# Attention slots of a six-layer windowed block: order, banks and the rotated product

## What is computed

```python
def attn_layer(x, Wqkv, qs, ksc, Wo):              # x shifted by one token in half of its features
    q, k, v = jnp.split(x @ Wqkv, 3, -1)           # 16 heads of 64
    q = l2norm(q) * qs;  k = l2norm(k) * ksc
    q = q * cos * scale + rotate_half(q) * sin * scale
    k = k * cos * inv + rotate_half(k) * sin * inv
    out = local_attention(q, k, v)                 # window 32, looks at itself and the window before
    return out.transpose(0, 2, 1, 3).reshape(b, n, INNER) @ Wo
...
for i in range(DEPTH):                             # DEPTH = 6
    x = attn_layer(shift_tokens(x), ...) + x
    x = ffn_layer(shift_tokens(x), ...) + x
```

## Time and profile before

| | us |
|---|---|
| median of 3 runs | 3929.46 (3925.46 to 3941.01) |
| span of the profiled execution | 3926.6 |
| TensorE matmuls busy | 3690.6 (94%) |
| VectorE busy | 3058.0 (78%) |
| GpSimd busy | 2597.4 (66%) |
| ScalarE busy | 2270.7 (58%) |

### The profile page before, as it was taken

How to read it: one execution, slowest core, us unless ns; L and a number is a source line. 1 busy time by engine, 2 the same in 40 slices (tenths; PEclk the granted TensorE clock), 3 DMA queues, 4 the chain that set the end, 5 groups by cost and what they waited for, 6 DMA issues and landing times.

```text
span 3926.6 us, 163773 instructions
## 1 busy us (share of the span) xinstructions
PE 3690.6 (94%) x67712; PEld 2844.7 (72%) x67712; DVE 3058.0 (78%) x5829; ACT 2270.7 (58%) x4270; POOL 2597.4 (66%) x3029
## 2 busy tenths in 40 slices
PE   5999979999999999999999999999999999999998
PEld 3555557777767777677877678787677876777876
DVE  7666658888778888788887788887788887888876
ACT  3555546666546666456666366665466664566653
POOL 4545538787547887367887288775477873687870
PEclk8999989999999999999999999999999999999999
DMA  1000002222212222122222122222122221222220
GB/s 44 4 6 4 6 28 68 56 60 60 58 32 59 59 57 59 41 49 60 61 57 56 30 65 57 59 61 58 32 60 58 59 56 41 54 57 58 60 52 22
DMA packets 136313, 189.08 MB, mean 48 GB/s; under 512 B 38006, under 2 KB 58484, under 8 KB 135412
## 3 DMA queue, kind: packets, MB, share of 16 engines
q1 hardware_dynamic: 135540, 178.23, 17.7%
HBM read 22.67 MB, written 2.10 MB: 6 GB/s over the span
## 4 chain that ended last, share of the span: by engine, by line
PE 76%; issue 4%; DVE 2%; POOL 2%; ACT 0%; DMA 0%; POOLq 0%; SPq 0%; DVEq 0%; ACTq 0%
PE PS L1270 18%; PE PS L1417 10%; PE PS L1256 10%; PE PS L1294 8%; PE PS L1280 8%; PE PS L1258 8%; PE PS L1257 8%; PE PS L1476 2%; PE PS L1411 2%; PE PS L1454 1%; PE PS L1447 1%; POOL t L1182 1%; PE PS L1442 1%; POOL t L1187 0%; DVE m L1800 0%
## 5 line engine op out<-in xcount | busy, mean ns | idle before, releaser
L1182 POOL TENSOR_TENSOR t<-t 128x1024 f32<-128x1024 f32 x384 | 908.0, 2370 | 363.9 <-DVE t L1762 362.6
L1187 POOL TENSOR_TENSOR t<-t,rn 128x1024 f32<-128x1024 f32 x384 | 723.6, 1905 | 29.8 <-POOL rn L150 27.3
L1542 ACT ACTIVATE va<-PS 128x512 f32<-128x512 f32 x384 | 229.8, 599 | 614.4 <-PE PS L1258 611.6
L1760 DVE TENSOR_TENSOR t<-PS,rope 128x512 f32<-128x512 f32 x768 | 523.2, 681 | 26.1 <-ACT sq L1577 24.5
L1256 PE MATMUL PS<-w_hi,xh 128*128 128x512 f32 x1152 | 514.2, 446 | 22.3 <-DVE xl L1063 11.3
L1577 ACT ACTIVATE sq<-PS 128x512 f32<-128x512 f32 x768 | 454.1, 593 | 33.0 <-PE PS L1258 17.7
L1270 PE MATMUL PS<-constants,t 128*128 128x128 f32 x3072 | 443.8, 277 | 19.8 <-POOL t L1187 12.8
L1258 PE MATMUL PS<-w_lo,xh 128*128 128x512 f32 x1152 | 458.5, 398 | 0.0
L1257 PE MATMUL PS<-w_hi,xl 128*128 128x512 f32 x1152 | 457.5, 397 | 0.0
L1767 DVE TENSOR_REDUCE ss<-sq 128x16 f32<-128x1024 f32 x384 | 448.3, 1209 | 0.0
L1270 PEld LDWEIGHTS PS<-constants,t 128*128 128x128 f32 x3072 | 351.9, 141 | 68.9 <-POOL t L1187 15.9
(11 more groups left out here) (168 smaller groups left out, 7869.8 us busy)
## 6 DMA issues: line engine op xcount, KB each, us to landing
vs<-va SPq DMA_DIRECT2D x768, 130.0 KB
vs<-va SPq DMA_DIRECT2D x768, 65.0 KB
t<-in_L_ffn_Wqkv SPq DMA_DIRECT2D x18, 512.0 KB, 4.4
w_out<-in_L_ffn_Wo SPq DMA_DIRECT2D x6, 512.0 KB, 3.9
a_normed<-in_L_attn_x SPq DMA_DIRECT2D x8, 256.0 KB, 7.0
a_xo<-in_L_attn_x SPq DMA_DIRECT2D x8, 256.0 KB, 2.8
out<-total SPq DMA_DIRECT2D x8, 256.0 KB, 3.5
w_raw<-in_L_ffn_W SPq DMA_DIRECT2D x6, 341.0 KB
```

The costliest lines, as they stand in the source:

```text
L1182: pool.tensor_tensor(mine[:, i, :], mine[:, i, :], t2[:, i, :], ALU.add).then_inc(done, 1)
L1187: pool.tensor_tensor(h, h, bc(rn[:, H * i:H * (i + 1)], 2, HB), ALU.mult).then_inc(done, 1)
L1760: dve.tensor_tensor(o1, src, bc(rope[:, 2 * i, t, :], 1, 8), ALU.mult)
```

## The change

The order on TensorE becomes k0, k1, v0, both halves of `turn_weights`, q0, q1, both of `turn_q`, both value products one behind the other, v1, both of `turn_k`, both of `turn_mixed`, the masks and all scores in one run, and the output projection last. Banks are fixed for each use: v0 in bank 1, v1 in 6, k in 4 and 5, q in 6 and 7, k transposed in 4 and 5, the mixed output transposed in 7 and 6, value products of half 0 in 2 and 3, of half 1 in 0 and 1, the output projection in 0. VectorE adds the output of a tile one slot later, ahead of the rotations, and `rope_half` makes the product with the sines in one operation that reads its source with the two halves of each head swapped (`swapped`). ScalarE's order follows. The diff, indentation reduced:

```diff
@@ -1291,7 +1291,7 @@
                 v = va[rows, room(s, t), par, pair, :] if k is None else vs[rows, t % 2, k, pair, :]
-                last = pe.matmul(PS[W * w:W * (w + 1), (0, 2)[c] + par, HB1 * (pair % 4):HB1 * (pair % 4 + 1)],
+                last = pe.matmul(PS[W * w:W * (w + 1), (2, 0)[c] + par, HB1 * (pair % 4):HB1 * (pair % 4 + 1)],
                                  pT[rows, pair, W * w:W * (w + 1)], v, start=True, stop=True,
@@ -1306,7 +1306,7 @@
     closing, ending = list(ages) == CLOSING, list(ages) == LAST
-    oT_at, y_at = (0, 2) if ending else (4, 4)
+    oT_at = (7, 6) if project_new else (0, 1)
     roped = lambda i: lambda j: t1[:, tile1 % 2, i, P * j:P * (j + 1)]
@@ -1322,41 +1322,47 @@
         pe.wait_ge(kn_made, at(T, 1, 1, 1))
-        if mix:
-            pe.wait_ge(on_made, at(T, 2, 2, 1))
-        turn(c, lambda j: roped(1)(4 * c + j), kt_mm)
+        pe.wait_ge(qT_made, at(T, 1, 2, c + 1))
+        turn(4 + c, lambda j: roped(1)(4 * c + j), kt_mm)
 
     def turn_mixed(c):
-        if score:
-            pe.wait_ge(qT_made, at(T, 1, 2, c + 1))
-        pe.wait_ge(on_made, at(T, 2, 2, c + 1))
-        turn(oT_at + c, lambda j: on[:, 4 * c + j, :, :].rearrange("p r d -> p (r d)"), ot_mm)
+        pe.wait_ge(on_made, at(T, 2, 2, c + 1 if project_new else 2))
+        if project_new and c == 0:
+            pe.wait_ge(rq_made, at(T, 0, 2, 2))
+        if project_new and c == 1:
+            pe.wait_ge(v_made, at(T, 0, 2, 2))
+        turn(oT_at[c], lambda j: on[:, 4 * c + j, :, :].rearrange("p r d -> p (r d)"), ot_mm)
 
     def mix_half(c):
-        pe.wait_ge(pT_made, at(T, 2, 2, c + 1))
+        pe.wait_ge(pT_made, at(T, 2, 2, 2))
+        if c == 1:
+            pe.wait_ge(attn_done, at(T, 3, 1, 1))
+            if project_new:
+                pe.wait_ge(v_made, at(T, 0, 2, 1))
         pe.sem_inc(pv_begun, 1)
...
 
-    def score_half(c):
+    def scores():
+        for par in range(2):
+            rows = slice(HB * par, HB * (par + 1))
+            pe.matmul(PS[:, 2 + par, :], sel_bf[rows, :], bc(mask_q[tile1][rows, :], 1, PAIRS),
+                      start=True, stop=False, skip_group_check=True)
         pe.wait_ge(carried, at(T, 1, 1, 1))
-        pe.wait_ge(qT_made, at(T, 1, 2, c + 1))
-        pe.wait_ge(kT_made, at(T, 1, 2, c + 1))
+        pe.wait_ge(qT_made, at(T, 1, 2, 2))
+        pe.wait_ge(kT_made, at(T, 1, 2, 2))
         pe.sem_inc(s_begun, 1)
-        return score_pairs(tile1, range(4 * c, 4 * (c + 1)))
+        score_pairs(tile1, range(PAIRS)).then_inc(s_mm, 1)
 
...
             pe.wait_ge(xl_made, 2 * halves(lay, s, t // 2) + 2)
-        pe.wait_ge(rq_made, at(T, 1, 2, 2))
-        project(2, 0, 7, t, v_mm)
         if s == 0 and t == 1:
             pe.wait_ge(rk_made, at(T, 1, 2, 2))
-    pe.wait_ge(attn_done, at(T, 3, 1, 1))
-    if project_new:
         project(1, 0, 4, t, k_mm)
         project(1, 1, 5, t, k_mm)
-        pe.wait_ge(v_made, at(T, 1, 2, 2))
-        project(0, 0, 6, t, q_mm)
+        if s == 0 and t == 1:
+            pe.wait_ge(ffn_done, lay * B + B)
+        project(2, 0, 1, t, v_mm)
     if closing:
@@ -1369,17 +1375,18 @@
         turn_weights(0)
+        turn_weights(1)
     if project_new:
-        pe.wait_ge(v_made, at(T, 0, 2, 1))
+        pe.wait_ge(v_made, at(T, 1, 2, 2))
+        project(0, 0, 6, t, q_mm)
+        pe.wait_ge(rq_made, at(T, 1, 2, 2))
         project(0, 1, 7, t, q_mm)
-    if mix:
-        turn_weights(1)
-        pe.wait_ge(vs_in[tile2 % 2], VS_IN * (lay * (B * 2) + s2 * 2 + tile2 // 2) + VS_IN)
-        mix_half(0)
     if score:
...
     if mix:
+        pe.wait_ge(vs_in[tile2 % 2], VS_IN * (lay * (B * 2) + s2 * 2 + tile2 // 2) + VS_IN)
+        mix_half(0)
         mix_half(1)
@@ -1391,9 +1398,8 @@
     if score:
-        if s == 0 and t == 1:
-            pe.wait_ge(ffn_done, lay * B + B)
         turn_k(0)
+        turn_k(1)
     if mix:
@@ -1404,21 +1410,14 @@
     if score:
-        turn_k(1)
-        pe.wait_ge(on_made, at(T, 2, 2, 2))
-        for par in range(2):
-            rows = slice(HB * par, HB * (par + 1))
-            pe.matmul(PS[:, 2 + par, :], sel_bf[rows, :], bc(mask_q[tile1][rows, :], 1, PAIRS),
-                      start=True, stop=False, skip_group_check=True)
-        score_half(0)
+        pe.wait_ge(on_made, at(T, 2, 2, 1))
+        scores()
     if mix:
...
         for pair in range(PAIRS):
-            last = pe.matmul(PS[:, y_at, 0:P], w_out[:, pair, :], oT[:, pair, :],
+            last = pe.matmul(PS[:, 0, 0:P], w_out[:, pair, :], oT[:, pair, :],
                              start=(pair == 0), stop=(pair == PAIRS - 1))
         last.then_inc(y_mm, 1)
-    if score:
-        score_half(1).then_inc(s_mm, 1)
 
@@ -1616,24 +1615,25 @@
         copy(kT[:, 1 - p, 4 * c:4 * (c + 1), W:],
-             PS[:, c, :].rearrange("p (j q) -> p j q", j=4)).then_inc(kT_made, 1)
+             PS[:, 4 + c, :].rearrange("p (j q) -> p j q", j=4)).then_inc(kT_made, 1)
 
...
 
+    oT_at = (7, 6) if 0 in ages else (0, 1)
     if ending:
         shift(lay, 1)
-    if 0 in ages:
-        values(lay, s, t, 0, 7)
-        square(T, 1, 0, 4, k_mm, sqk_made)
     if 2 in ages:
...
     if 0 in ages:
+        square(T, 1, 0, 4, k_mm, sqk_made)
+    if 2 in ages:
+        weigh(1)
+    if 0 in ages:
         square(T, 1, 1, 5, k_mm, sqk_made)
     if 2 in ages:
-        weigh(1)
         turned_weights(0)
@@ -1641,6 +1641,7 @@
         square(T, 0, 1, 7, q_mm, sqq_made)
+        values(lay, s, t, 0, 1)
     if 1 in ages:
@@ -1648,18 +1649,17 @@
         turned_k(0)
+        turned_k(1)
     if 2 in ages:
...
             act.wait_ge(ot_mm, at(T, 2, 2, c + 1))
-            pairs(oT, c, (0 if ending else 4) + c, oT_made)
+            pairs(oT, c, oT_at[c], oT_made)
         if ending:
...
             gate(lay, 0, 0, 2)
-    if 1 in ages:
-        turned_k(1)
     if 0 in ages:
@@ -1749,6 +1749,9 @@
 
+def swapped(a):
+    return bass.AP(a.tensor, a.offset + 32, [list(a.ap[0]), [64, 8], [-32, 2], [1, 32]])
+
 def rope_half(T, t, i, c, bank, squared, turned, added, done):
@@ -1758,8 +1761,8 @@
     dve.tensor_tensor(o1, src, bc(rope[:, 2 * i, t, :], 1, 8), ALU.mult)
-    dve.tensor_tensor(o2[:, :, 0:32], src[:, :, 32:64], bc(rope[:, 2 * i + 1, t, 0:32], 1, 8), ALU.mult)
-    dve.tensor_tensor(o2[:, :, 32:64], src[:, :, 0:32], bc(rope[:, 2 * i + 1, t, 32:64], 1, 8),
+    dve.tensor_tensor(o2.rearrange("p h (a d) -> p h a d", a=2), swapped(PS[:, bank, :]),
+                      bc(rope[:, 2 * i + 1, t, :].rearrange("p (a d) -> p a d", a=2), 1, 8),
                       ALU.mult).then_inc(done, 1)
@@ -1806,6 +1809,8 @@
                               bc(m[:, :, js], 3, 2 * W), ALU.subtract).then_inc(e_made, 1)
+    if s * TPS + t >= 3:
+        add_output(lay, T, 3, before(s, t, 3))
     if closing:
@@ -1816,13 +1821,14 @@
         rope_half(T, t, 0, 0, 6, sqq_made, qt_mm, addq_made, rq_made)
+        rope_half(T, t, 0, 1, 7, sqq_made, qt_mm, addq_made, rq_made)
     if 2 in ages:
...
             dve.wait_ge(ot_mm, at(T, 3, 2, c + 1))
-            bank = (0, 2)[c]
+            bank = (2, 0)[c]
             o = PS[:, bank:bank + 2, 0:4 * HB1].rearrange("p r (j e) -> p r j e", e=HB1)
@@ -1830,20 +1836,21 @@
     if 0 in ages:
-        rope_half(T, t, 0, 1, 7, sqq_made, qt_mm, addq_made, rq_made)
         lengths(T)
...
             hidden(lay, 0, 0, j)
-    if 2 in ages:
-        dve.wait_ge(y_mm, at(T, 2, 1, 1))
-        dve.wait_ge(ffn_done, lay * B + s2 + 1)
-        now = state[:, bass.ds(s2, 1), 1 + P * tile2:1 + P * (tile2 + 1)]
-        dve.tensor_tensor(now, PS[:, 2 if ending else 4, 0:P].unsqueeze(1), now, ALU.add).then_inc(attn_done, 1)
-    if ending:
+        add_output(lay, T, 2, (s2, tile2))
         hidden(lay, 0, 0, 2)
+
+def add_output(lay, T, back, place):
+    s, tile = place
+    dve.wait_ge(y_mm, at(T, back, 1, 1))
+    dve.wait_ge(ffn_done, lay * B + s + 1)
+    now = state[:, bass.ds(s, 1), 1 + P * tile:1 + P * (tile + 1)]
+    dve.tensor_tensor(now, PS[:, 0, 0:P].unsqueeze(1), now, ALU.add).then_inc(attn_done, 1)
 
```

## The result

The changed kernel takes 4169.63 us (median of 4 runs, 4163.79 to 4187.33), the kernel before 3927.46 us (4 runs, 3924.84 to 3941.01) beside it on the same chip. The ratio is 1.0612, with a 95% interval from 1.0591 to 1.0633: slower by 242 us, where the prediction had 168. The direction holds and the time lies within the range. The term for the pauses came out at its size, in part by luck, and one term is missing.

The account below looks back on a forecast made before the run. TensorE bounds the kernel, running out of instructions in dense runs. Changes of form -0.4 and pauses +1.3 give +0.9 us a slot, times 187 = 168 us on 3926.6; forecast 4096 us, range 3985 to 4185.

Parts of the forecast that it names:

- The term for the pauses: TensorE's waits for instructions in the merged value and score runs grow by 1.3 us a slot, between 1.0 and 1.65.
- What bounds it: TensorE, matmuls busy 94% of the span, runs out of instructions in dense runs; these pauses cost about 0.6 us a slot.
- The changes of form: On TensorE, fewer entries into and exits from value products and scores save 0.4 us a slot, between 0.3 and 0.6.
- the delay of 3.2 us from the 40th load: On TensorE, the next instruction block is ready 3.2 us after about the 40th load of the running block.
- The scaling down by a quarter: Old-order working gave 0.77 us against 0.55 to 0.6 measured, so new-order pauses of 2.2 us became 1.6; 1.9 taken.
- VectorE, banks and waits: Swapped product saves VectorE 0.55 us a slot, uncounted; bank reuse and new TensorE waits count nothing, 0.3 kept for range.
- tight: Softmax work of about 3.8 us is covered by w_out and nine projection matmuls, 4.1 us; uncovered, up to 0.3 a slot.
- The signs: Profile: "issue" pauses up to 2.3 us, some 125 loads apart, about 350 us on two lines; undisturbed slot 13.3 to 13.5.
- (1): Instruction supply costs merged runs no more than now; only changes of form are saved, -75 us, 3855 us; chance 0.08.
- (2): Instruction delay nearer 2.6 us, or sequencer further ahead: pauses grow 0.6 to 0.9 us a slot, 3970 to 4020; chance 0.14.
- the 0.05 for an end within 0.5%: Chance 0.05 that the whole kernel's time stays within 0.5% of now, given as the low end of the shorter-delay rival.
- (3): VectorE becomes second bound through a slow swapped read or late value normalisation: some 0.4 us a slot, 4170 or above; chance 0.1.

Follow-up runs that it names:

- the kernel with both merges: The kernel before with turn_q ahead of both value halves and w_out behind both score halves, nothing else of the change: 4117.44 us, ratio 1.0475.
- The step within the scores: The changed kernel with three long-met waits and one unread semaphore increment between the two score halves: 4153.7 us, ratio 1.0567.
- values merged: The kernel before with the transposes of q ahead of both value halves, which become one run of 128 loads: 4011.64 us, ratio 1.0191.
- scores merged: The kernel before with w_out behind both score halves instead of between them: 4061.63 us, ratio 1.0329.
- The same work spread out: The kernel before with v1 between turn_q and the second value half, both turn_k ahead of turn_mixed, VectorE and ScalarE reordered, rotated product in one operation: 3882.68 us.

## Why the prediction was right, and where it was not

**What bounds it.** Right. TensorE's busy time did not move and the span did. That the pauses are the supply of instructions was argued from three views and is now shown: with data, order and neighbours kept, they moved when only the place of the block moved (from none to 170 in the value products). One count in this part is wrong and carries nothing: a slot has 32 transposes, not 24, which makes up the 324 loads.

**The changes of form.** -0.4 us a slot, the slot without pauses at 13.4. Measured 13.35: -0.45, within the bounds. It does not come from where it was put, though. The turned q and both value halves take 2.61 us before and 2.60 after, so that the merge of the values saved nothing, and the kernel with that merge alone has 13.78 us for its shortest slots. Scores and w_out went from 3.56 to 3.33, as expected. The other 0.21 us are in the projections and the turned weights (4.67 to 4.46), where the new order has both halves of turn_weights side by side; the sum had nothing for that.

**The pauses.** The growth was to be 1.3 us a slot, 243 us over 187 slots. Measured 322.1 - 86.9 = 235 us. That agreement is partly luck. The longest pause was to be 2.25 us and is 3.0. The step that was off is the delay of 3.2 us from the 40th load, taken from two pauses of the old order. In the trace the packet starts a median of 0.63 us behind the 40th load in the kernel before and 0.79 us in the change (0.92 for its pauses above 2 us). It takes 1.05 and 1.12 us, and the loads resume 1.43 and 1.39 us behind its end. So it is 3.1 us before and 3.3 to 3.4 in the change. The number of pauses was too high in the working: 83 of 125 places over 187 slots are 124 pauses for each run, 1.7 us on average (1.13 x 125 / 83). There came 78 in the scores, 2.27 us on average, and 57 in the value products, 1.99. Fewer and longer gave about the same sum. The scaling down by a quarter had no mechanism behind it. A full slot takes 15.52 us on average after and 14.49 before, so that all time beyond the undisturbed one is 2.17 us a slot, against 0.69. Not scaled, the working had 2.2 and 0.77. It was scaled to the pauses in two lines, 0.55 to 0.6 us, although the same text reads 0.86 us of longer slot from rows 2.

At this place the Trainium skill, Runtime: NRT & Kernel Launch, section Instruction fetch mechanics, has the crossing into the next block mostly hidden. The trace disagrees, with 2.50 us of idle loads around one packet. The block of 256 instructions, on the other hand, agrees: counted in the trace's records of TensorE's queue, 132 of the 162 distances from one pause over 0.9 us to the next are exact multiples of 256 in the change, and 15 more are off by one.

**VectorE, banks and waits.** Nothing in the sum, and nothing was found: the swapped product takes 681 ns, its kernel 0.9993 of the time before. The note that the softmax has about 3.8 us of work under 4.1 us of cover, "tight", was right and matters more than it seemed: the two experiments that put w_out back between the scores of the changed kernel have 187.0 and 188.5 us of waits there, where the change has 7.2.

**The term that is missing** is TensorE's clock. The prediction reads the granted clock once (1.00) and gives it no term. Long pauses are followed by stretches at 1.2 GHz, in which w_out takes 2.75 us instead of 1.81. Half-clock time grew by 225.9 - 50.1 = 176 us. Were all of it filled with TensorE's work, taken to need twice as long there, this would cost 88 us, and it is an upper bound. The busy time points to nearly as much: with slots shorter by 84 us in all it should have fallen by that, and it fell by 0.8.

**The sum again.** Pauses +235, the shorter slot -0.45 x 187 = -84, the clock up to +88: +239 at most, where the spans differ by 235. By the same terms the prediction had +243 - 75 = +168. So the pauses' size was met and their consequence was not. The fit to 4 us is no proof of the terms, since the clock is in it at its bound and the 30 us more in the transposes are not in it. By place the prediction had +168 for 187 slots and nothing elsewhere; measured are +201 in the slots and +34 outside them, where 43 us of the added half-clock time lie.

**The signs.** Pauses with the reason "issue", multiples of a block apart, and the undisturbed slot are as foretold. The pauses in the two lines are 290 us, not 350. VectorE's wait for w_out has not gone but is 40.5 us, and its wait for value products did not grow: 99.7 us, where the kernel before has 121.1.

**The rivals.** (1), 3855 us, is refuted: the merges cost. (2), a shorter delay, is refuted by the packets, as it was longer; the 0.05 for an end within 0.5% did not follow from it either, since its own low end, 3970 us, is 1.0% above 3929. (3) gave the right neighbourhood, 4170, by the wrong mechanism.

**What stays open.** That the two merges alone make the kernel 4.75% slower is shown, and that the pauses are the supply of instructions. Why the change, with the same two runs, has 157 us more of pauses and 84 us more of half-clock time is not shown; its undisturbed slot, 0.87 us shorter, hides that in the time. In the kernel with both merges the packet starts 0.39 us behind the 40th load, in the change 0.79. Which of the change's other edits moves the packet isn't known. The step within the scores did not, and other transfers are not needed for it, as the packet at 1090.25 had the DMA engines to itself. No run changed the clock alone: that long pauses bring it down is argued from what stands ahead of the stretches. The table does not settle it (values merged has fewer pauses than scores merged, and more half-clock time), and not every long pause does it.

## What to carry to other kernels

Before small matmuls are put in one run, ask the trace how fast they use up a block of instructions: here 64x32 products go at some 12 ns a load with its matmul, a block of 256 in 1.5 us, and the next one needs over 3. Leave longer operations between them. The same work spread out gained 1.5%; gathered in two runs it lost 4.75%.
A pause on TensorE has two prices, its length and the slower clock behind it; count both.
Before work is moved out of or into a run, look at which chain it covers where it stands: w_out was a pad within the scores and, moved behind them, the cover of the softmax.

## What the runs showed of the hardware

- A block of instructions of TensorE is 256 long, comes as one packet (0.02 MB, about 1.1 us), and its first instruction is executed 1.4 us behind the packet's end, in all kernels measured here (medians 1.38 to 1.45).
- At the pauses of the unpadded kernels the next packet starts, in the median, only 0.4 to 0.9 us behind the 40th load of the running block, with 107 of 256 instructions left in the kernel before and 49 in the change; in the change's pauses above 2 us a median of 20 was left.
- A semaphore increment on TensorE's queue is 51 ns in the trace and is not hidden between long matmuls: 19,000 of them made the kernel 1810 us longer, up to 1031 us of it by the lower clock (granted 0.80 in the mean, 0.965 in the change).
- VectorE reads a PSUM source with its halves swapped at the full pace: 681 ns for 128x512, where the plain product has 686.
- The granted clock fell to its lower level 57 times in the change, for 3.4 us (47 times) or 6.8 us (9), 54 times during or within 3.5 us behind an idle time of 1.8 us or more.
